# Masked attention of a four-layer network on one core: the order of TensorE's products inside a position, front units cut in two, and a second layer that seeds both pairs

## The chip, the core and the metric

The program runs on one core of a Trainium2 chip. The core has TensorE (PE), which multiplies matrices into PSUM, VectorE (DVE), ScalarE (ACT), GpSimd (POOL), and SyncE (SP), which here only issues DMAs. Each engine works through its own list of instructions in order; semaphores let one wait for another. The metric is the device time of one execution in microseconds (us), lower is better.

## The reference

The network has four layers, each an attention block and a feed-forward block. Batch 8, 512 tokens, width 256, 16 heads of 16. Layers 0, 1 and 3 have a masked cross attention; these three are what the change touches. For each of them:

```
Q = heads(norm(x) @ Wq + bq);  K = heads(ctx @ Wk + bk);  V = heads(ctx @ Wv + bv)
scores = Q @ K^T / sqrt(16)        # layer 1: + adj[query, key]
scores = where(mask == 0, very negative, scores)
x = x + softmax(scores) @ V @ Wo + bo
```

Layers 0 and 1 have a mask for each batch element, layer 3 one mask for all; layer 1 adds a matrix `adj` of floats to the scores.

## The kernel before

`masked_attention` (called three times) keeps x in SBUF and loops over the 8 batch elements ("batches" below; two of them are one turn of a hardware loop, the first and last ones are written out). A batch is cut into NG = 4 groups of GH = 4 heads, and a group into 4 blocks of 128 keys: 16 **steps** s, each with two halves, so 32 **positions** p = 2s + half. Every engine walks the same positions, in `pe_positions`, `dve_positions`, `act_positions`; POOL and SP have a frame for each batch. What stands at a position is fixed by hand.

At each position TensorE does, for two of the four heads:

- two **maxima products** (`p1_ps[0]`, `p1_ps[1]`; L280), 128 queries by 512 keys, seven steps ahead of the rest. VectorE adds the mask and takes the row maximum of each (L452, one instruction and a short read of its accumulator). There are only these two banks: a product may start when the maximum of the product two before it is done (semaphore `maxed`).
- two **score products** (`p2_ps[half]`, L293), 128 keys by 512 queries, with the maximum already subtracted inside the product through three extra rows of `q_stack`. The mask is added in one of three ways. By ACT: it **seeds** the two banks with the mask (`act_seed`, L512) before the product, which adds on top. By PE: two more products with the identity after it (L298), layers 0 and 3. By DVE: it adds the mask while copying to `probs` (L467), layer 1. Then ACT takes the exponential (L535).
- at odd positions the four **value products** of the step before (L308, f32, into `oT_ps`).

Between these stand **front units** in one bank `front_ps`: transposes of the normed x (`xT`), projections `k`, `q`, `v` for a later batch, the output projection `out` of the batch before, and `m`, which turns the maxima of a group (split in three bf16 parts by `dve_split_maxima`) so that they can be put into `q_stack`. The tables `VALUES`, `FRONT`, `TAIL`, `MAXIMA` say at which position; ACT or DVE reads a unit one position later, ahead of its other work there. A batch has 10 units of the five kinds and 4 of `m`.

Which half is seeded by whom, before:

```python
def by_act(s, half):
    return half == 0 or s % 2 == 1
def by_dve(s, half):
    return adj is not None and not by_act(s, half)
def by_pe(s, half):
    return adj is None and not by_act(s, half)
```

So of the 32 position pairs of a batch 24 are seeded by ACT; the eight at half 1 of even steps go by PE (layers 0 and 3) or DVE (layer 1).

The program's own functions follow.

## Time and profile before

| | |
|---|---|
| median of 3 runs | 3940.72 us (3933.82 to 3943.34) |
| the profiled execution's own time | 3939.15 us |
| its span, first to last instruction | 3937.3 us |
| PE busy over the span | 3204.4 us (81%) |
| DVE busy | 2542.3 us (65%) |
| ACT busy | 2278.4 us (58%) |
| POOL busy | 1118.4 us (28%) |
| masked attention of layer 0, 1, 3 | about 60 to 700, 1060 to 1756, 2880 to 3516 us of the span |
| its value products (L308) | 3072, 422.3 us busy |
| its maxima on DVE (L452) | 1536, 1003.9 us busy |

The kernel has stages with different limits, so the shares over the span say little. The change lies in the three stages of masked attention, half of the time. In them the granted clock of TensorE was 0.93 to 0.98 of full speed.

In the rows below, "L280 ... x2" in a timeline is a run of equal instructions merged into one row; the first number is its start in us from the start of the span, the second how long it took. A matmul's duration holds its way through the array, so for the time that it takes from the next one, compare starts. In square brackets stands how long the engine was idle before, and what ended that.

### The profile page before, as it was taken

The page shows a single profiled execution, that of the slowest core. Times are in us where ns is not written, and L with a number is a line of the kernel's source. Part 1 is how long each engine was busy: PE and PEld are TensorE (multiplying, and loading weights), DVE is VectorE, ACT ScalarE, POOL GpSimd, SP SyncE. Part 2 cuts the span into 40 slices and gives each one's busy share as a digit, 9 for nine tenths or more (in the row PEclk, how much of TensorE's full clock was granted, in tenths as well). Part 3 has the DMA queues.
Part 4 walks back from the last instruction along what each step waited for, and adds up shares of the span by engine and source line. Part 5 has one row for each costly group of instructions (what it writes and reads, how often), then busy time and mean ns, then how long its engine had stood idle before and what let it go on. Part 6 is the DMA issues. An engine that isn't in the chain of part 4 may idle for free. (4 is left out here: it accounts for less than half of the span.)

```text
span 3937.3 us, 66613 instructions
## 1 busy us (share of the span) xinstructions
PE 3204.4 (81%) x16721; PEld 1523.3 (39%) x16721; DVE 2542.3 (65%) x7732; ACT 2278.4 (58%) x3034; POOL 1118.4 (28%) x1194
## 2 busy tenths in 40 slices
PE   5888888799578888876997888888379889866897
PEld 2333332344222322224653555555123333225565
DVE  4776776677578788755215777888867777745531
ACT  1887879444177677762114666676538888861111
POOL 3344431000444455401112432331332211101232
PEclk8999999899799999977998999998589999985899
DMA  5322330000343333301007988997031221103242
GB/s 143 82 66 69 84 76 18 22 1 0 100 108 96 89 92 89 84 9 48 0 15 245 305 286 278 312 325 262 24 79 39 49 66 41 34 12 107 69 101 67
DMA packets 212154, 392.83 MB, mean 100 GB/s; under 512 B 24633, under 2 KB 76986, under 8 KB 211658
## 3 DMA queue, kind: packets, MB, share of 16 engines
q1 hardware_dynamic: 168777, 296.38, 27.1%
q10 hardware_dynamic: 36864, 83.90, 5.7%
q0 software_dynamic: 6144, 8.39, 1.3%
q8 instruction: 139, 2.28, 0.2%
q14 instruction: 230, 1.88, 0.2%
HBM read 189.88 MB, written 96.47 MB: 73 GB/s over the span
## 5 line engine op out<-in xcount | busy, mean ns | idle before, releaser
L452 DVE CUSTOM_DVE_ANT_0 A_sums<-A_p_ps,A_bias 128x512 bf16<-128x512 f32 x1536 | 1003.9, 685 | 366.1 <-PE A_p_ps L280 348.8
L535 ACT ACTIVATE A_probs<-A_p_ps 128x1024 f32<-128x1024 f32 x704 | 715.0, 1017 | 191.5 <-PE A_p_ps L293 152.5
L280 PE MATMUL A_p_ps<-A_k_stack,A_q_stack 96*128 96x512 bf16 x1536 | 538.0, 396 | 231.1 <-DVE A_nmax L452 221.9
L512 ACT ACTIVATE A_p_ps<-A_biasT 128x1024 f32<-128x1024 bf16 (+1 forms) x576 | 592.0, 1028 | 73.7 <-ACT A_probs L535 2.9
L293 PE MATMUL A_p_ps<-A_q_stack,A_k_stack 99*128 99x512 bf16 x1536 | 473.6, 391 | 41.2 <-ACT A_p_ps L512 39.2
L308 PE MATMUL A_oT_ps<-A_probs,A_v_aug 128*17 128x512 f32 x3072 | 422.3, 623 | 0.5 <-ACT A_probs L535 0.5
L280 PEld LDWEIGHTS A_p_ps<-A_k_stack,A_q_stack 96*128 96x128 bf16 x1536 | 131.6, 98 | 723.6 <-DVE A_nmax L452 626.0
L1107 DVE CUSTOM_DVE_ANT_0 A_scores<-A_qk_ps,A_rel_in 128x384 f32<-128x384 f32 (+3 forms) x512 | 232.6, 486 | 83.3 <-PE A_qk_ps L991 72.0
L1014 PE MATMUL A_t_ps<-ident,A_scores 128*128 128x128 f32 x1280 | 226.5, 298 | 57.2 <-DVE A_probsT L1097 47.4
L1097 DVE COPY A_probsT<-A_t_ps 128x384 f32<-128x384 f32 (+3 forms) x512 | 229.0, 484 | 54.3 <-PE A_t_ps L1014 45.6
L1162 ACT ACTIVATE A_rel_out<-A_rel_ps 128x1024 f32<-128x1024 f32 (+3 forms) x256 | 180.1, 704 | 141.7 <-PE A_rel_ps L980 132.6
L1169 ACT ACTIVATE A_scores<-A_scores,A_nmax 128x384 f32<-128x384 f32 (+3 forms) x512 | 257.5, 555 | 7.6 <-DVE A_nmax L1107 7.5
L293 PEld LDWEIGHTS A_p_ps<-A_q_stack,A_k_stack 99*128 99x128 bf16 x1536 | 144.3, 99 | 207.2 <-ACT A_p_ps L512 77.2
L1189 POOL TENSOR_SCALAR_AFFINE_SELECT A_rel_in<-A_rel_in 128x256 f32<-128x256 f32 x256 | 102.6, 410 | 386.5 <-DMA A_rel_in<-A_rel_dram 383.8
L1014 PEld LDWEIGHTS A_t_ps<-ident,A_scores 128*128 128x128 f32 x1280 | 151.0, 148 | 133.9 <-DVE A_probsT L1097 56.4
L582 POOL TENSOR_SCALAR A_bias<-A_mask_in 128x512 bf16<-128x512 int32 (+2 forms) x68 | 131.4, 1933 | 217.2 <-DVE A_nmax L452 196.1
L582 POOL TENSOR_SCALAR A_biasT<-A_mask_in 128x512 bf16<-128x512 int32 (+2 forms) x68 | 131.1, 1927 | 205.9 <-DVE A_probs L467 82.5
L1524 PE MATMUL B_cv_ps<-B_hs,B_tap_diag 128*128 128x512 f32 x384 | 179.0, 602 | 2.7 <-DVE B_hs L1626 2.7
L2780 ACT ACTIVATE M_hid<-M_h_ps,M_b 128x512 f32<-128x512 f32 x64 | 44.0, 688 | 189.6 <-PE M_h_ps L2582 189.6
L2099 ACT ACTIVATE U_hid<-U_h_ps,U_hid_bias 128x512 f32<-128x512 f32 x64 | 44.0, 687 | 177.6 <-PE U_h_ps L1937 177.6
L991 PE MATMUL A_qk_ps<-A_k_stack,A_q_stack 96*128 96x384 bf16 (+3 forms) x512 | 126.7, 312 | 13.8 <-DVE A_nmax L1107 12.2
L561 POOL CAST A_parts<-A_qk 128x512 bf16<-128x512 f32 x84 | 51.2, 609 | 297.0 <-ACT A_qk L497 296.6
(345 smaller groups left out, 5407.5 us busy)
## 6 DMA issues: line engine op xcount, KB each, us to landing
A_k_stack<-A_parts SPq DMA_DIRECT2D x192, 256.0 KB, 5.0
A_q_stack<-A_parts SPq DMA_DIRECT2D x192, 256.0 KB, 5.2
A_rel_dram<-A_rel_out ACTq DMA_DIRECT2D x64, 512.0 KB, 5.1
A_rel_in<-A_rel_dram SPq DMA_DIRECT2D x64, 512.0 KB, 5.0
A_rel_dram<-A_rel_out ACTq DMA_DIRECT2D x64, 384.0 KB, 4.1
A_rel_in<-A_rel_dram SPq DMA_DIRECT2D x64, 384.0 KB, 5.2
A_ctxT<-in_ctxT SPq DMA_DIRECT2D x32, 512.0 KB, 6.3
A_mask_in<-in_mask SPq DMA_DIRECT2D x64, 256.0 KB, 4.4
```

The lines of the kernel that those rows point to most:

```text
L280: nc.tensor.matmul(p1_ps[i % 2][:, :], q_stack[0:KS, a_par, j * GH + i, t * P:(t + 1) * P], k_stack[0:KS, a_par, j * GH + i, :], start=Tru ...
L293: last = nc.tensor.matmul(p2_ps[half][:, i % 2, :], k_stack[:, par, j * GH + i, kb * P:(kb + 1) * P], q_stack[:, par, j * GH + i, :], star ...
L308: nc.tensor.matmul(oT_ps[CW * i:CW * i + HD + 1, :], v_aug[:, v_par, kb, j * GH + i, :], probs[:, (s - 1) % 2 * 2 + i // 2, i % 2, :], sta ...
L452: nc.vector.tensor_tensor_reduce(out=sums[:, i % NX, :], in0=p1_ps[i % 2][:, :], in1=bias[:, t, :], scale=-1.0, scalar=3.4028235e38, op0=A ...
L512: nc.scalar.activation(p2_ps[half][:, :, :], turned, ACT.Copy).then_inc(seeded, 1)
L535: nc.scalar.activation(dst, src, ACT.Exp).then_inc(exp_done, 1)
L582: last = nc.gpsimd.tensor_scalar(dst, mask_in[:, k % 2, :], 0.0, NEG, ALU.is_equal, ALU.mult)
L1014: last = nc.tensor.transpose(t_ps[:, i, kb, :], scores[(p - TURN_LAG) % NP][:, i, kb * P:(kb + 1) * P], ident[:, :])
L1097: nc.vector.tensor_copy(probsT[u % NP][:, i, 0:nk, :], t_ps[:, i, 0:nk, :]).then_inc(copied, 1)
L1107: nc.vector.tensor_tensor_reduce(out=scores[p % NP][:, i, 0:n], in0=qk_ps[i][:, 0:n], in1=rel_in[s % NI][:, (2 * half + i) * n:(2 * half + ...
L1162: nc.scalar.activation(rel_out[a % NO][:, 2 * half * n:(2 * half + 2) * n].rearrange("p (i n) -> p i n", i=2), rel_ps[:, :, 0:n], ACT.Copy ...
L1169: nc.scalar.activation(scores[u % NP][:, i, 0:n], scores[u % NP][:, i, 0:n], ACT.Exp, bias=nmax[:, u % NP, i:i + 1], scale=-1.0).then_inc( ...
```

## The change

Four things, all in the masked layers.

1. TensorE's order inside a position. Before: both maxima products, scores, values, front unit. Now: first maxima product, scores, first half of a front unit, an `m` unit if one is due, second maxima product, second half of the front unit, values.
2. A front unit is cut into two pieces of 256 columns (`piece`), and reported as full after the second. `k` and `q` units were products with 512 moving columns and are now twice as many with 256; the others keep their instructions.
3. The tables move: all ten units now stand at even positions (before, `v` 0 and 1 at 1 and 5, `xT` 1 at 15, `q` 0 at 25). `END` goes from 12 to 14 with `out` 1.
4. Layer 1: `by_act` is always true. ACT seeds the eight pairs that DVE used to add the mask to, DVE's addition (L467) and the semaphore `biased` go, and ACT reads scores from PSUM at every position. Layers 0 and 3 keep their eight pairs by PE.

```diff
 def by_act(s, half):
-    return half == 0 or s % 2 == 1
+    return adj is not None or half == 0 or s % 2 == 1
...
-VALUES = [(1, "v", 0), (5, "v", 1)]
-FRONT = [(12, "xT", 0), (15, "xT", 1), (18, "k", 0), (20, "k", 1), (25, "q", 0), (28, "q", 1)]
-TAIL = [(8, "out", 0), (10, "out", 1)]
+VALUES = [(0, "v", 0), (4, "v", 1)]
+FRONT = [(14, "xT", 0), (16, "xT", 1), (20, "k", 0), (22, "k", 1), (24, "q", 0), (28, "q", 1)]
+TAIL = [(8, "out", 0), (12, "out", 1)]
...
 # pe_shared
-for c in range(DC):
-    last = nc.tensor.matmul(front_ps[:, :], wt[:, c, i * P:(i + 1) * P], src[:, c, :],
+cols = slice(piece * D, (piece + 1) * D)
+for c in range(DC):
+    last = nc.tensor.matmul(front_ps[:, cols], wt[:, c, i * P:(i + 1) * P], src[:, c, cols],
                             start=c == 0, stop=c == DC - 1)
...
+if piece == 1:
+    last.then_inc(front_full, 1)
...
 # pe_positions, one position
+if has(b, a):
+    pe_max_unit(pe, b, a, a_par, 2 * half)
+if has(b, s):
+    pe_scores(pe, b, s, half, par)
+for n, kind, i in here:
+    pe_shared(pe, n, kind, i, uses_before(b), b, 0)
+for n, kind, i in shared(plan, p):
+    if kind == "m":
+        pe_maxima(pe, n, i, uses_before(b), b)
+if has(b, a):
+    pe_max_unit(pe, b, a, a_par, 2 * half + 1)
+for n, kind, i in here:
+    pe_shared(pe, n, kind, i, uses_before(b), b, 1)
 if half == 1 and has(b, s - 1):
+    pe_values(pe, b, s, par)
...
 # dve_positions
-if has(b, s) and by_dve(s, half):
-    dve.wait_ge(p2_done, b * HALVES + p + 1).then_inc(apart_dve, 1)
-    nc.vector.tensor_tensor(probs[:, s % 2 * 2 + half, :, :], p2_ps[half][:, :, :], turned, ALU.add).then_inc(biased, 1)
...
 # act_positions: at every position now
+act.wait_ge(p2_done, b * HALVES + p + 1).then_inc(apart_act, 1)
+nc.scalar.activation(probs[:, s % 2 * 2 + half, :, :], p2_ps[half][:, :, :], ACT.Exp).then_inc(exp_done, 1)
```

TensorE in layer 0, batch 0, from position 18 on: `p1_ps` are the maxima banks, `p2_ps` the scores, `oT_ps` the values, `front_ps` the front bank (here a `k` unit and an `m` unit). Before:

```order
L280 MATMUL A0_p1_ps0<-A0_k_stack,A0_q_stack 128x512
L280 MATMUL A0_p1_ps1<-A0_k_stack,A0_q_stack 128x512
L293 MATMUL A0_p2_ps0<-A0_q_stack,A0_k_stack 128x512 x2
L241 MATMUL A0_front_ps<-A0_ctxT,A0_wk 128x512 x2
L280 MATMUL A0_p1_ps0<-A0_k_stack,A0_q_stack 128x512
L280 MATMUL A0_p1_ps1<-A0_k_stack,A0_q_stack 128x512
L293 MATMUL A0_p2_ps1<-A0_q_stack,A0_k_stack 128x512 x2
L308 MATMUL A0_oT_ps<-A0_probs,A0_v_aug 17x512 x4
L252 MATMUL A0_front_ps<-ident_bf,A0_m_parts 12x128 x4
```

After, positions 18, 19 and the start of 20:

```order
L261 MATMUL A0_p1_ps0<-A0_k_stack,A0_q_stack 128x512
L276 MATMUL A0_p2_ps0<-A0_q_stack,A0_k_stack 128x512 x2
L261 MATMUL A0_p1_ps1<-A0_k_stack,A0_q_stack 128x512
L261 MATMUL A0_p1_ps0<-A0_k_stack,A0_q_stack 128x512
L276 MATMUL A0_p2_ps1<-A0_q_stack,A0_k_stack 128x512 x2
L251 MATMUL A0_front_ps<-ident_bf,A0_m_parts 12x128 x4
L261 MATMUL A0_p1_ps1<-A0_k_stack,A0_q_stack 128x512
L292 MATMUL A0_oT_ps<-A0_probs,A0_v_aug 17x512 x4
L261 MATMUL A0_p1_ps0<-A0_k_stack,A0_q_stack 128x512
L276 MATMUL A0_p2_ps0<-A0_q_stack,A0_k_stack 128x512 x2
L230 MATMUL A0_front_ps<-A0_ctxT,A0_wk 128x256 x2
L261 MATMUL A0_p1_ps1<-A0_k_stack,A0_q_stack 128x512
```

The scores moved between the two maxima products, the `m` unit moved from behind the values to ahead of the second maxima product, and the `k` unit went two positions on and is cut: half of it stands ahead of the second product, the other half behind.

ScalarE at the start of layer 1 (`A1_p2_ps0`, `A1_p2_ps1` are the banks of half 0 and 1; L512 seeds, L535 is the exponential). Before:

```order
L535 ACTIVATE A1_probs<-A1_p2_ps0 128x1024
L512 ACTIVATE A1_p2_ps0<-A1_biasT 128x1024
L535 ACTIVATE A1_probs<-A1_probs 128x1024
L512 ACTIVATE A1_p2_ps1<-A1_biasT 128x1024
L535 ACTIVATE A1_probs<-A1_p2_ps0 128x1024
L512 ACTIVATE A1_p2_ps0<-A1_biasT 128x1024
L535 ACTIVATE A1_probs<-A1_p2_ps1 128x1024
```

After (L529 is the exponential):

```order
L529 ACTIVATE A1_probs<-A1_p2_ps0 128x1024
L512 ACTIVATE A1_p2_ps0<-A1_biasT 128x1024
L529 ACTIVATE A1_probs<-A1_p2_ps1 128x1024
L512 ACTIVATE A1_p2_ps1<-A1_biasT 128x1024
L529 ACTIVATE A1_probs<-A1_p2_ps0 128x1024
L512 ACTIVATE A1_p2_ps0<-A1_biasT 128x1024
L529 ACTIVATE A1_probs<-A1_p2_ps1 128x1024
L512 ACTIVATE A1_p2_ps1<-A1_biasT 128x1024
```

Every exponential is now followed by a seed, and none reads `probs` that DVE wrote.

## Rows read from the trace of the kernel before

**Rows 1.** Windows (layers 1, 3): length, busy PE, PEld, DVE, ACT, POOL; clock, DMA

```profile
1060.00:1756.00 696.00, 561.96 (x2557) 184.03 (x2555) 534.21 (x1472) 507.60 (x553) 306.13 (x246) 0.93 0.30 80
2880.00:3516.00 636.00, 553.78 (x2696) 196.81 (x2696) 437.67 (x1378) 505.22 (x554) 133.89 (x136) 0.98 0.19 43
```

**Rows 2.** Timeline of PE in layer 3: a step without a unit, then one

```profile
3205.46 0.61 PE L280 MATMUL A_p_ps<-A_k_stack,A_q_stack 96*128 96x512 bf16 x2
...
3206.80 0.39 PE L280 MATMUL A_p_ps<-A_k_stack,A_q_stack 96*128 96x512 bf16 x1 [0.29 <-DVE A_nmax L452]
3207.41 0.39 PE L280 MATMUL A_p_ps<-A_k_stack,A_q_stack 96*128 96x512 bf16 x1 [0.22 <-DVE A_nmax L452]
3207.64 0.60 PE L293 MATMUL A_p_ps<-A_q_stack,A_k_stack 99*128 99x512 bf16 x2
...
3208.60 1.05 PE L308 MATMUL A_oT_ps<-A_probs,A_v_aug 128*17 128x512 f32 x8
3209.58 1.98 PE L241 MATMUL A_front_ps<-A_xnT,A_wq 128*128 128x512 f32 x4
3211.40 0.60 PE L280 MATMUL A_p_ps<-A_k_stack,A_q_stack 96*128 96x512 bf16 x2
```

**Rows 3.** Timeline in layer 3: from a maxima product to its maximum and back

```profile
3187.45 0.60 PE L280 MATMUL A_p_ps<-A_k_stack,A_q_stack 96*128 96x512 bf16 x2
...
3188.02 0.69 DVE L452 CUSTOM_DVE_ANT_0 A_sums<-A_p_ps,A_bias 128x512 bf16<-128x512 f32 x1 [1.30 <-PE A_p_ps L280]
...
3188.78 0.39 PE L280 MATMUL A_p_ps<-A_k_stack,A_q_stack 96*128 96x512 bf16 x1 [0.30 <-DVE A_nmax L452]
```

**Rows 4.** Timeline of ACT in layer 3: seed, exponential, seed

```profile
3189.82 1.03 ACT L512 ACTIVATE A_p_ps<-A_biasT 128x1024 f32<-128x1024 bf16 x1
3190.79 1.02 ACT L535 ACTIVATE A_probs<-A_p_ps 128x1024 f32<-128x1024 f32 x1
3191.93 1.03 ACT L512 ACTIVATE A_p_ps<-A_biasT 128x1024 f32<-128x1024 bf16 x1
```

**Rows 5.** Timeline of ACT: the `oT_ps` copy, a batch apart (layers 3, 1)

```profile
3175.73 0.58 ACT L524 ACTIVATE A_oT_sb<-A_oT_ps 128x512 f32<-128x512 f32 x1
...
3252.20 0.58 ACT L524 ACTIVATE A_oT_sb<-A_oT_ps 128x512 f32<-128x512 f32 x1
...
1378.11 0.58 ACT L524 ACTIVATE A_oT_sb<-A_oT_ps 128x512 f32<-128x512 f32 x1
...
1461.77 0.58 ACT L524 ACTIVATE A_oT_sb<-A_oT_ps 128x512 f32<-128x512 f32 x1
...
1543.65 0.58 ACT L524 ACTIVATE A_oT_sb<-A_oT_ps 128x512 f32<-128x512 f32 x1
```

**Rows 6.** The same copy, one group apart, in layer 3's last batch

```profile
3421.68 0.58 ACT L524 ACTIVATE A_oT_sb<-A_oT_ps 128x512 f32<-128x512 f32 x1
...
3437.75 0.58 ACT L524 ACTIVATE A_oT_sb<-A_oT_ps 128x512 f32<-128x512 f32 x1
```

**Rows 7.** Timeline of DVE in layer 3: second maximum of a position, split's end

```profile
3192.85 0.68 DVE L452 CUSTOM_DVE_ANT_0 A_sums<-A_p_ps,A_bias 128x512 bf16<-128x512 f32 x1
...
3193.67 0.19 DVE L406 TENSOR_TENSOR A_m_parts<-A_m_rest,A_m_parts 128x16 bf16<-128x16 f32 x1
```

**Rows 8.** Timeline of PE, layer 3: a whole `v` unit

```profile
3228.48 2.00 PE L247 MATMUL A_front_ps<-A_wv,A_ctxT 128*128 128x256 f32 x8
```

**Rows 9.** Groups by line, layer 3: the weight loads of the `v` units

```profile
L247 PEld LDWEIGHTS A_front_ps<-A_wv,A_ctxT 128*128 128x128 f32 x112 | 20.8, 195 | 13.7 <-issue 11.3
```

**Rows 10.** Waits of ACT in layer 1, longest first: us in total, times, longest

```profile
ACT A_probs L535 <- DVE A_probs L467: 84.4, 59, 4.0
```

**Rows 11.** Waits of PE: in us, times, longest; layer 1, then layer 3

```profile
PE A_p_ps L280 <- DVE A_nmax L452: 94.5, 198, 2.3
PE A_p_ps L293 <- ACT A_p_ps L512: 23.7, 40, 2.4
...
PE A_p_ps L280 <- DVE A_nmax L452: 64.2, 197, 1.0
```

More of the change, by code:

```diff
@@ L173, in masked_attention @@
         START = 7
-        END = 12
+        END = 14
         def plan_of(b):
@@ new lines, in pe_max_unit, with pe_scores @@
+        def pe_max_unit(pe, b, a, a_par, i):
+            unit = (b * STEPS + a) * GH + i
+            _, _, j, t = ahead(a - LEAD)
+            if later(unit - 1):
+                pe.wait_ge(maxed, unit - 1)
+            nc.tensor.matmul(p1_ps[i % 2][:, :], q_stack[0:KS, a_par, j * GH + i, t * P:(t + 1) * P],
+                             k_stack[0:KS, a_par, j * GH + i, :], start=True, stop=True).then_inc(p1_done, 1)
+        def pe_scores(pe, b, s, half, par):
+            j, kb = s // TPB, s % TPB
+            pair = (2 * half, 2 * half + 1)
+            if half == 0 and kb == 0:
+                pe.wait_ge(m_placed[j % 2], (b * (NG // 2) + j // 2 + 1) * GH * 16)
+            if every_mask and s < TPB and not by_act(s, half):
+                pe.wait_ge(bias_ready, b * MK + TPB + kb + 1)
+            if by_act(s, half):
+                pe.wait_ge(seeded, seeds(b, s, half))
+            elif later(b * STEPS + s):
+                pe.wait_ge(exp_done, b * HALVES + 2 * s + half - 1)
+            for i in pair:
+                last = nc.tensor.matmul(p2_ps[half][:, i % 2, :], k_stack[:, par, j * GH + i, kb * P:(kb + 1) * P],
+                                        q_stack[:, par, j * GH + i, :], start=not by_act(s, half), stop=by_act(s, half),
+                                        skip_group_check=by_act(s, half))
+            if not by_act(s, half):
+                for i in pair:
+                    last = nc.tensor.matmul(p2_ps[half][:, i % 2, :], ident_bf[:, :], biasT[:, kb, :],
+                                            start=False, stop=True)
+            last.then_inc(p2_done, 1)
@@ new lines, in pe_values @@
+        def pe_values(pe, b, s, par):
+            j, kb = (s - 1) % STEPS // TPB, (s - 1) % TPB
+            v_par = par if s else 1 - par
+            pe.wait_ge(exp_done, b * HALVES + 2 * s)
+            if kb == 0 and later(b * NG + (s - 1) // TPB):
+                pe.wait_ge(oT_read, b * NG + (s - 1) // TPB)
+            for i in range(GH):
+                nc.tensor.matmul(oT_ps[CW * i:CW * i + HD + 1, :], v_aug[:, v_par, kb, j * GH + i, :],
+                                 probs[:, (s - 1) % 2 * 2 + i // 2, i % 2, :],
+                                 start=kb == 0, stop=kb == TPB - 1).then_inc(pv_done, 1)
@@ L311, in pe_positions @@
-                for n, kind, i in shared(plan, p):
-                    pe_shared(pe, n, kind, i, uses_before(b), b, par)
+                a_par = (par + over) % 2
+                if has(b, a) and half == 0 and a % STEPS == 0:
+                    for stack in stack_ready:
+                        pe.wait_ge(stack, (b + over + 1) * SLOTS * 16)
+                here = [(n, kind, i) for n, kind, i in shared(plan, p) if kind != "m"]
+                if has(b, a):
+                    pe_max_unit(pe, b, a, a_par, 2 * half)
```

112 lines of the change are left out of this document (25 added, 87 removed).

## The prediction

> **What bounds the kernel now.** I read first the windows of the masked layers, since the shares over the whole span mix stages: in layer 3 PE is busy 553.8 of 636 us and ACT 505.2, in layer 1 PE 562.0, DVE 534.2 and ACT 507.6 of 696 [rows 1]. No engine is full, so the limit is a mix of PE's work and of waits between engines. The waits of PE name the partner: 64.2 us in layer 3 and 94.5 in layer 1 for a maximum on DVE, against 23.7 for a seed of ACT in layer 1 [rows 11].
>
> The timeline of a step without a front unit shows the mechanism [rows 2]. From 3205.46, where its even position starts, to 3209.58, where its values have been issued, it takes 4.12 us. PE's own issue in it is less. A product of 512 columns takes 0.23 from start to start (3207.41 to 3207.64); two scores and two mask products take 0.96 (to 3208.60), the values 0.98 (to 3209.58). Four maxima products, two more scores, 0.96 and 0.98 are 3.27 us at 0.22 each. The other 0.85 are waits: a maxima product may start only when DVE is done with the product two before. That round trip is read from three rows: the product is issued at 3187.45, its maximum starts on DVE at 3188.02 (0.57), and 0.76 later, at 3188.78, PE issues into the freed bank [rows 3]. So a bank turns in 1.33 us, and DVE's pitch is 0.67 to 0.69 for one maximum. A bare even position (two maxima, two scores) is only 0.88 long. The first maxima product of the odd position waits 0.45 for the 1.33; the second stands right behind it and waits again until the next maximum is done, 0.69 later: 0.45 more, less rounding. By this count a bare step is 4.10 us, where the trace has 4.12. A front unit at the even position, 1.82 long (3209.58 to 3211.40 for one at an odd position [rows 2]), covers this wait; one at an odd position doesn't.
>
> A whole batch takes 76.47 us in layer 3 (3175.73 to 3252.20), in layer 1 83.66 and 81.88, mean 82.8 [rows 5].
>
> **The change, layers 0 and 3.** (a) With the new order the second maxima product comes 0.66 behind the first, at the pace of DVE, and finds its bank free. The first one of the odd position still waits 0.45. A bare step falls by 0.4.
>
> (b) By the tables, the steps with no unit of 1.8 us at their even position are ten now (0 to 3, 7, 8, 11, 12, 13, 15): 10 x 0.85 = 8.5 us of waits. After, they are 1, 3, 5, 9, 13, 15 at 0.45, and 7 and 8, where a short `xT` unit brings the even position to about 1.3, at nothing: 2.7. That removes 5.8 us from a batch.
>
> (c) Given back: the `m` unit now stands ahead of a maxima product instead of behind the values. It needs the end of the split. From the start of the second maximum to that end is 3193.67 + 0.19 - 3192.85 = 1.01 [rows 7]; that maximum starts 1.36 after the even position's start, so the unit may start at 2.43. PE is there at 1.33 + 0.22 + 0.5 = 2.05. A wait of 0.4, four times: 1.6. Before, the values (0.98) stood there and hid it; queued behind it now are the second maxima product, which DVE waits for, and the values.
>
> (d) ACT becomes late where PE no longer is. Seed to exponential is 0.97, exponential to the next seed 1.14 [rows 4]. A step with two seeds is 2 x 2.11 = 4.2 and a copy of some 0.5 (the 0.58 of [rows 5], less overlap). Step 8 is shorter than that on PE (about 3.75), steps 10 and 14 about equal: 1.0 together.
>
> (e) The cuts. PE goes from bf16 to f32 and back twice as often; about 0.08 is what 0.96 has over four products of 0.22, where PE changes to f32 [rows 2]. Ten more changes at half of that: 0.5.
>
> (f) `k` and `q` units have twice the weight loads. I cost them at nothing: a `v` unit, eight products of 256 columns, takes 2.00 [rows 8], a `q` unit, four of 512, takes 1.98 [rows 2]; the cover is the product in flight. Without cover it would be one load of 0.195 [rows 9] for each.
>
> The Trainium skill ("TensorE: Matmul & The Clock Gate", section "The mechanism" of Part 3) says that a weight load overlaps products in flight only if it goes to another group of rows. Here all loads of a unit use all 128 rows; by that rule the `v` unit's eight loads would add 1.6 us to its products, and the trace doesn't show them.
>
> Sum for a batch: -5.8 + 1.6 + 1.0 + 0.5 = -2.7; the waits behind DVE's other work (norm, heads, splits) I take as unchanged. Six batches of each of the two layers have front units: 12 x 2.7 = 32 us. The last two batches have fewer. A group there takes 16.07 [rows 6], where ACT's own work is six seeds with their exponentials at 2.11, two single exponentials of about 1.0 and two copies at 0.5: 15.7. That leaves 0.4 to gain in a group, 16 x 0.4 = 6 us. Together 38.
>
> **Layer 1.** DVE loses 64 additions, for which ACT waited 84.4 us [rows 10]; ACT gains 64 seeds of 0.97 to 1.14. ACT then has 32 x 2.11 = 67.5 in a batch and 14 copies at 0.5: 74.5, more than PE (no mask products: eight times 0.43 less than in layer 3). It is the bound. Where single steps on PE are still longer (an even step with unit, 4.7 against 4.2) and round DVE's heavy stretch (norm, two heads, `out` at positions 6 to 9) I add 4: 78.5, against 82.8 now. 6 x 4.3 = 26 us; in the last two batches, already short, nothing. The bounds are 0 and 82.8 - 74.5 = 8.3 for a batch.
>
> **Total:** 38 + 26 = 64 us less than the profiled execution's 3939.15 is 3875; the median of the runs lies 1.6 above it, so I say 3877.
>
> **Rivals.**
> *Everything removed stays removed* (chance 0.16). If splits are ready and ACT smooths its load over neighbouring steps, (c) to (e) vanish: 5.8 x 12 + 6 = 76, and layer 1 at 76.5 gives 38. That is 114 us: 3827. For it: steps with much ACT work stand beside ones with little. Against: each score product needs its own seed, so ACT can be late by one position at most.
> *Given back in full* (0.08). DVE's heavy stretch had a unit at position 10 behind it, which gave DVE 1.8 us to catch up; now positions 9 to 11 are bare. If that and the split cost 2.5 more for a batch in all three layers, about 45 are lost: 3922 or more, down to no difference.
> *The weight loads are not hidden* (0.04). 28 units of `k` and `q` in the loops of each layer, four more loads each: 84 x 4 x 0.195 = 66 us. Then 3943: no gain. Against it speaks (f). By the rule of the Trainium skill named in (f) it is this case that would come.
> *Slower: the second maxima product queues behind the scores* (0.08). A score product that waits for its seed now holds up half of DVE's supply; before, both maxima products were ahead of it. PE waited for seeds only 40 times, 23.7 us, in layer 1 [rows 11], but with ACT as the bound there it would wait at nearly all positions, and PE gets to the scores 0.22 earlier than before. A maximum that is late by w makes the next position late by up to w. Over 768 positions it costs 768 w; at w = 0.08 us the gain is gone, at 0.12 it gives 3877 + 92 = 3969. Against: from the end of a seed to the moment when ACT wants that score lie an exponential and a seed, 2.1 us, and PE needs about 0.7 for the scores.
>
> **How the numbers follow.** The forecast, 3850 to 3910, has 0.64. The range reaches from the first rival (3827, and a little of it is left out below) into the second: 3828 to 3926. Above lie the last two and part of the second, together about 0.16. A change within 0.3% (12 us) can hardly be told from none here. Faster: 0.64 + 0.16 + a third of the second, 0.83. Same: the rest of the second and the third, 0.09. Slower: 0.08.
>
> **What would show it.** Right: PE's waits for a maximum fall by more than half in all three layers, and a bare step shows one such wait, not two; the batch in layer 3 is at 73.8; `k` and `q` units cut in two are 0.9 + 0.9 long; in layer 1 ACT is the busiest, with the batch at 78.5 and no exponential waiting for DVE. Wrong: PE's waits move to the seeds (scores) and to the split (`m` unit) with sizes above 0.4; DVE is idle as long as before; weight loads show between the halves; the stretch round positions 6 to 11 grows by more than what the bare steps give.

## The result, and the profile after

| | before | after |
|---|---|---|
| median of the runs on one chip | 3938.4 us (3933.82 to 3943.34) | 3868.81 us (3864.12 to 3871.64) |
| ratio, 95% interval | | 0.9822 [0.9805, 0.9839] |
| span of the profiled execution | 3937.3 us | 3862.4 us |
| PE, DVE, ACT busy | 3204.4, 2542.3, 2278.4 us | 3166.3, 2497.0, 2330.4 us |

The change makes the kernel 70 us faster (1.8%); 64 was predicted. Medians and ratios here and below are those of executions in the faster of the chip's two states; one execution of the kernel before, at 4764.6 us, was in the slower one. The windows of layers 1 and 3, with the columns of [rows 1]:

```profile
1021.00:1695.00 674.00, 552.30 (x2672) 211.00 (x2672) 470.31 (x1413) 566.71 (x617) 310.66 (x248) 0.93 0.31 84
2820.00:3442.00 622.00, 550.47 (x2808) 218.37 (x2808) 453.67 (x1378) 501.70 (x554) 131.38 (x135) 0.97 0.19 44
```

Both stages are shorter. In layer 1 ACT is now the busiest (566.7 of 674), as forecast; DVE lost 64 us there. In layer 3 PE and ACT are as busy as before. DVE is busy for 16 us more (437.7 to 453.7): 11 of them are at the maxima (335.0 to 346.0), which take as long each (686 and 687 ns, about 351 us for all 512) but whose records overlap less now that they no longer follow each other directly, and the rest are other instructions of DVE that lasted longer.

To split the 75 us of the span by stage I take ScalarE's copies of `oT_ps`, 32 in each masked layer, one for each group. Here are the first and the last of layer 1 and of layer 3 after the change:

```profile
1077.61 0.58 ACT L524 ACTIVATE A_oT_sb<-A_oT_ps 128x512 f32<-128x512 f32 x1
1694.20 0.60 ACT L524 ACTIVATE A_oT_sb<-A_oT_ps 128x512 f32<-128x512 f32 x1 [1.25 <-PE A_oT_ps L292]
2879.16 0.58 ACT L524 ACTIVATE A_oT_sb<-A_oT_ps 128x512 f32<-128x512 f32 x1
3441.32 0.60 ACT L524 ACTIVATE A_oT_sb<-A_oT_ps 128x512 f32<-128x512 f32 x1 [1.25 <-PE A_oT_ps L292]
```

From the first to the last copy layer 1 takes 616.6 us and layer 3 562.2. The same marks in both traces give:

| from mark to mark | before | after | difference |
|---|---|---|---|
| start of the span to layer 0's first | 114.4 | 105.5 | -8.9 |
| layer 0, first to last | 585.8 | 557.2 | -28.6 |
| on to layer 1's first | 417.2 | 414.9 | -2.3 |
| layer 1 | 638.3 | 616.6 | -21.7 |
| on to layer 2's first | 395.2 | 393.0 | -2.2 |
| layer 2 (not changed) | 611.4 | 617.3 | +5.9 |
| on to layer 3's first | 181.7 | 174.7 | -7.0 |
| layer 3 | 571.2 | 562.2 | -9.0 |
| on to the end | 422.1 | 421.1 | -1.0 |

A stage moves by 3 to 7 us between kernels that have the same code in it: layer 2 lay between 611.1 and 618.3 in all traces of this study, and among six kernels with the same code in layers 0 and 3, layer 0 lay between 555.8 and 558.7 and layer 3 between 555.4 and 559.6. Differences of that size are not read as effects. Below, a kernel's "length of layer 0, 1, 3" is this first-to-last length in its profiled execution.

Every fourth copy begins another batch. The mean of the first six batches, and the length of the last two together, in us:

| | layer 0 | layer 1 | layer 3 |
|---|---|---|---|
| a batch, mean of six, before | 79.4 | 85.9 | 76.8 |
| after | 74.6 | 82.3 | 75.3 |
| the last two together, before | 109.5 | 123.1 | 110.6 |
| after | 109.5 | 123.0 | 110.6 |

All that the masked layers gained lies in the first six batches.

PE's waits in layer 1 after the change (us in total, times, longest), against [rows 11]:

```profile
PE A_p_ps L261 <- DVE A_nmax L460: 41.1, 79, 2.1
PE A_p_ps L276 <- ACT A_p_ps L512: 33.0, 43, 1.5
PE A_front_ps L251 <- DVE A_m_parts L414: 27.8, 20, 2.7
PE A_front_ps L230 <- ACT A_m_row L490: 9.1, 7, 2.1
```

And in layer 3:

```profile
PE A_p_ps L261 <- DVE A_nmax L460: 35.4, 77, 1.5
PE A_p_ps L276 <- ACT A_p_ps L512: 10.3, 16, 1.5
PE A_front_ps L251 <- DVE A_m_parts L414: 9.9, 23, 1.1
...
PE A_front_ps L230 <- ACT A_m_row L490: 5.2, 6, 0.9
```

The waits for a maximum fell by 57% in layer 1 (94.5 to 41.1) and by 45% in layer 3 (64.2 to 35.4), in number from 198 and 197 to 79 and 77. A part came back: as waits of the `m` unit for the split, in layer 1 for seeds, and as waits of a front unit that stands directly behind an `m` unit until ACT has read the bank (between the first and the last copy of layer 3, all kinds of units together, 7.4 us against 0.4 before). The timeline of a step without a unit in layer 3 after the change, with the start of the next one:

```profile
3151.86 0.39 PE L261 MATMUL A_p_ps<-A_k_stack,A_q_stack 96*128 96x512 bf16 x1
3152.08 0.60 PE L276 MATMUL A_p_ps<-A_q_stack,A_k_stack 99*128 99x512 bf16 x2
3152.52 0.38 PE L261 MATMUL A_p_ps<-A_k_stack,A_q_stack 96*128 96x512 bf16 x1
3153.19 0.39 PE L261 MATMUL A_p_ps<-A_k_stack,A_q_stack 96*128 96x512 bf16 x1 [0.29 <-DVE A_nmax L460]
...
3153.85 0.38 PE L261 MATMUL A_p_ps<-A_k_stack,A_q_stack 96*128 96x512 bf16 x1
3154.16 1.05 PE L292 MATMUL A_oT_ps<-A_probs,A_v_aug 128*17 128x512 f32 x8
3155.56 0.39 PE L261 MATMUL A_p_ps<-A_k_stack,A_q_stack 96*128 96x512 bf16 x1 [0.35 <-DVE A_nmax L460]
```

Inside the step there is one wait, at the first maxima product of the odd position, where [rows 2] had two. The second product of each position starts without one. (This step has no mask products, the one of [rows 2] has them.)

### The profile page after: what moved, and what is told of

It reads as the page before. It is cut to its first block and busy times, and to the rows that moved or that the text cites. A ratio compares the mean times of both kernels' runs of the same rounds, so it can differ in the third digit from the quotient of the medians.

```text
span 3862.4 us, 67385 instructions
## 1 busy us (share of the span) xinstructions
PE 3166.3 (82%) x17105; PEld 1598.6 (41%) x17105; DVE 2497.0 (65%) x7668; ACT 2330.4 (60%) x3098; POOL 1118.6 (29%) x1194
## 5 line engine op out<-in xcount | busy, mean ns | idle before, releaser
L460 DVE CUSTOM_DVE_ANT_0 A_sums<-A_p_ps,A_bias 128x512 bf16<-128x512 f32 x1536 | 1036.0, 687 | 443.7 <-PE A_p_ps L261 405.2
L529 ACT ACTIVATE A_probs<-A_p_ps 128x1024 f32<-128x1024 f32 x768 | 777.7, 1015 | 175.5 <-PE A_p_ps L281 76.7
L512 ACT ACTIVATE A_p_ps<-A_biasT 128x1024 f32<-128x1024 bf16 (+1 forms) x640 | 657.6, 1028 | 77.9 <-ACT A_probs L529 3.7
L261 PE MATMUL A_p_ps<-A_k_stack,A_q_stack 96*128 96x512 bf16 x1536 | 603.4, 395 | 119.9 <-DVE A_nmax L460 112.0
L261 PEld LDWEIGHTS A_p_ps<-A_k_stack,A_q_stack 96*128 96x128 bf16 x1536 | 149.4, 97 | 646.0 <-DVE A_nmax L460 562.3
L1100 DVE CUSTOM_DVE_ANT_0 A_scores<-A_qk_ps,A_rel_in 128x384 f32<-128x384 f32 (+3 forms) x512 | 232.4, 486 | 88.2 <-PE A_qk_ps L984 82.8
```

The costliest lines, as they stand in the source:

```text
L261: nc.tensor.matmul(p1_ps[i % 2][:, :], q_stack[0:KS, a_par, j * GH + i, t * P:(t + 1) * P], k_stack[0:KS, a_par, j * GH + i, :], start=Tru ...
L460: nc.vector.tensor_tensor_reduce(out=sums[:, i % NX, :], in0=p1_ps[i % 2][:, :], in1=bias[:, t, :], scale=-1.0, scalar=3.4028235e38, op0=A ...
L512: nc.scalar.activation(p2_ps[half][:, :, :], turned, ACT.Copy).then_inc(seeded, 1)
L529: nc.scalar.activation(probs[:, s % 2 * 2 + half, :, :], p2_ps[half][:, :, :], ACT.Exp).then_inc(exp_done, 1)
L1100: nc.vector.tensor_tensor_reduce(out=scores[p % NP][:, i, 0:n], in0=qk_ps[i][:, 0:n], in1=rel_in[s % NI][:, (2 * half + i) * n:(2 * half + ...
```

## The experiments

All were run in five rounds, in turn with the kernel before: the first four of the list below the change beside a median of before of 3936.5 us, the next four beside 3939.7, the last four beside 3940.3 (the change itself beside 3938.4). Medians, ratios to before with their 95% intervals, and the lengths of the three layers:

| kernel | median us | ratio | layer 0 | layer 1 | layer 3 |
|---|---|---|---|---|---|
| before | 3938.4 | | 585.8 | 638.3 | 571.2 |
| the change | 3868.8 | 0.9822 [0.9805, 0.9839] | 557.2 | 616.6 | 562.2 |
| seed_only | 3917.6 | 0.9949 [0.9932, 0.9967] | 584.8 | 618.0 | 574.2 |
| dve_adds | 3970.6 | 1.0085 [1.0065, 1.0105] | 563.3 | 704.2 | 565.8 |
| old_order | 3871.0 | 0.9836 [0.9811, 0.9860] | 562.4 | 613.1 | 563.4 |
| old_tables | 3881.4 | 0.9856 [0.9833, 0.9878] | 566.1 | 605.8 | 573.4 |
| m_last | 3855.1 | 0.9792 [0.9764, 0.9819] | 556.6 | 613.5 | 559.6 |
| uncut | 3864.8 | 0.9806 [0.9781, 0.9831] | 556.2 | 617.5 | 558.9 |
| cut_c | 3865.5 | 0.9816 [0.9791, 0.9841] | 560.6 | 619.3 | 562.8 |
| m_last_l1old | 3839.3 | 0.9746 [0.9719, 0.9772] | 556.0 | 592.5 | 555.5 |
| nan_late_l1old | 3836.3 | 0.9748 [0.9727, 0.9769] | 558.7 | 591.9 | 555.5 |
| q_late | 3847.5 | 0.9766 [0.9746, 0.9787] | 556.5 | 609.8 | 555.4 |
| v_late | 3845.0 | 0.9760 [0.9739, 0.9781] | 556.5 | 600.0 | 555.5 |
| nan_late | 3855.1 | 0.9788 [0.9767, 0.9809] | 555.8 | 611.1 | 555.4 |

Across these groups I compare ratios, and medians only within one.

### The seeding alone, and all but the seeding

`seed_only` is the kernel before with one line of the change (and without POOL's wait for `biased`, which nothing raises any more):

```diff
-return half == 0 or s % 2 == 1
+return adj is not None or half == 0 or s % 2 == 1
```

> The kernel before with nothing but layer 1's seeding changed. Theory A: about 26 us faster than the kernel before, about 3912, all in layer 1, where ACT becomes the busiest engine. Rival: with the old order, ACT as the bound and PE waiting for maxima add up, and nothing is gained (3935 to 3942).

`dve_adds` is the changed kernel with that line as it was (and DVE's addition, its semaphore and POOL's wait for it back):

```diff
-return adj is not None or half == 0 or s % 2 == 1
+return half == 0 or s % 2 == 1
```

> The changed kernel with layer 1's eight pairs of a batch added by VectorE again (L467 back, ACT seeds 24). Theory A: layer 1 gives back the 26 us that the prediction gave it, about 3895; layers 0 and 3 don't move. Rival: layer 1's gain is the order's, and the 64 seeds on ACT cost as much as the 64 additions on VectorE did: within 5 us of the changed kernel, or faster.

Alone, the seeding shortens layer 1 by 20 us (638.3 to 618.0). But with the new order and without the seeding, layer 1 takes 704.2, which is 88 longer than after the change and 66 longer than before, and the kernel is slower than before. Its waits in layer 1:

```profile
ACT A_probs L553 <- DVE A_probs L485: 148.7, 59, 5.9
PE A_p_ps L271 <- DVE A_nmax L470: 75.4, 66, 5.5
PE A_p_ps L286 <- ACT A_p_ps L530: 64.3, 63, 2.8
```

ACT waits 148.7 us for DVE's additions, against 84.4 before [rows 10]. DVE makes the addition behind the second maximum of the position, and TensorE now issues that product behind the scores; when a score product waits for its seed, the second maximum, the addition, the exponential and the next seed all come later, one after the other. PE's waits for seeds are 64.3 us, against 23.7 before [rows 11]. (The longest single wait, 5.9 us, is no example of it: 3.0 of it are idle time of DVE ahead of the addition for which the trace shows no reason.) This fits the chain that I had as the slower rival, and with the seeding layer 1 doesn't show it: two parts of the change that looked separate are not. That it is the new order that does this, and not the new places, is argued from the lists; no run has DVE's additions with only one of the two.

### The order and the tables, one without the other

`old_order` is the changed kernel with both maxima products first and the pieces of a unit back to back behind the values, with the `m` unit after them:

```diff
 if has(b, a):
     pe_max_unit(pe, b, a, a_par, 2 * half)
+    pe_max_unit(pe, b, a, a_par, 2 * half + 1)
 if has(b, s):
     pe_scores(pe, b, s, half, par)
-for n, kind, i in here:
-    pe_shared(pe, n, kind, i, uses_before(b), b, 0)
...
-if has(b, a):
-    pe_max_unit(pe, b, a, a_par, 2 * half + 1)
-for n, kind, i in here:
-    pe_shared(pe, n, kind, i, uses_before(b), b, 1)
 if half == 1 and has(b, s - 1):
     pe_values(pe, b, s, par)
+for n, kind, i in here:
+    for piece in range(2):
+        pe_shared(pe, n, kind, i, uses_before(b), b, piece)
...
```

> The changed kernel with TensorE's old order inside a position: both maxima products, scores, values, the two halves of the front unit back to back, the m unit. Tables and seeding stay new. Theory A (the change pays by sparing waits for a maximum on VectorE): each bare step has its second wait of about 0.4 us again, eight of them in a batch, and the m unit's wait of about 0.4 (four in a batch) goes; about 25 us slower than the changed kernel, near 3894, with PE's waits for a maximum back above 50 us in each layer. Theory B (the new places of the units do nearly all of it): at most 5 us slower. Theory C (seeding in layer 1 does nearly all): layers 0 and 3 as in the changed kernel.

`old_tables` is the changed kernel with the places of before:

```diff
-VALUES = [(0, "v", 0), (4, "v", 1)]
-FRONT = [(14, "xT", 0), (16, "xT", 1), (20, "k", 0), (22, "k", 1), (24, "q", 0), (28, "q", 1)]
-TAIL = [(8, "out", 0), (12, "out", 1)]
-END = 14
+VALUES = [(1, "v", 0), (5, "v", 1)]
+FRONT = [(12, "xT", 0), (15, "xT", 1), (18, "k", 0), (20, "k", 1), (25, "q", 0), (28, "q", 1)]
+TAIL = [(8, "out", 0), (10, "out", 1)]
+END = 12
```

> The changed kernel with the old places of the front units (and END 12). Order, cuts and seeding stay new. Theory A: steps whose even position is bare are ten again, at 0.45 us each instead of six at 0.45 and two at nothing: 1.8 us for a batch, 18 batches, some 25 to 30 us slower than the changed kernel, about 3896. Theory B (places do nearly all): 40 us or more slower in layers 0 and 3 together. Rival: order alone does it, at most 5 us slower.

From `seed_only` (0.9949) the order alone (with the cuts and the `m` unit's move) leads to 0.9856, the tables alone to 0.9836, both to 0.9822: 37, 45 and 50 us of some 3940. So the two are largely substitutes; the 5 us between 45 and 50 are within the intervals. Of the theories for `old_order`, A (25 us slower) fell and B's number came (at most 5 slower, 5.5 by the ratios), but not as B reads it, since the places aren't needed for most of the gain: the order alone gives 37. `old_tables` is 13 us slower by the ratios, half of its theory A.

Each of the two puts PE's other work into the gap that DVE needs between maxima, and a gap can be filled once. PE's waits for a maximum between the first and the last copy of layer 3 show this: 54.1 us in `seed_only`, 30.4 with the order alone, 40.3 with the tables alone, 27.0 with both. But in layer 3 the order alone brings only 1 us of time (574.2 to 573.4), the tables 11 (to 563.4), although the order takes away more of these waits. `old_tables` has others in their place, in layer 3:

```profile
PE A_p_ps L261 <- DVE A_nmax L460: 30.4, 88, 1.0
...
PE A_front_ps L251 <- ACT A_qk L497: 9.3, 6, 1.6
PE A_front_ps L251 <- DVE A_m_parts L414: 8.3, 14, 1.3
PE A_front_ps L251 <- DVE x_sb L394: 5.1, 7, 1.1
```

The `m` unit (L251) comes earlier in the new order, while the old places put `out` 1 and `k` 0 directly ahead of it: it waits 14.4 us for their bank to be read and 8.3 for the split, 22.7 of the 23.7 us that the maxima gave. So in layer 3 the order's small gain may be a matter of the bank and not of the gap; the old places with the `m` unit behind the values were run in layer 1 only (`m_last_l1old`). In layer 0 the order brings 19, the tables 22, both 28. In layer 1 the old places are better by 11 us than the new ones (605.8 against 616.6): there this part of the change seems to cost time, and the runs below make it clearer.

### The two halves of a unit

`uncut` issues the whole front unit behind the second maxima product:

```diff
-for n, kind, i in here:
-    pe_shared(pe, n, kind, i, uses_before(b), b, 0)
...
 for n, kind, i in here:
-    pe_shared(pe, n, kind, i, uses_before(b), b, 1)
+    for piece in range(2):
+        pe_shared(pe, n, kind, i, uses_before(b), b, piece)
```

> The changed kernel with the whole front unit in one place, behind the second maxima product and ahead of the values (the products of k and q units still 256 wide). My theory, that what the order brings comes from the scores between two maxima products and not from the cut: within 8 us of the changed kernel (3861 to 3877). Rival: the half unit ahead of the second maxima product is what gives DVE its evenly spaced products; then PE's waits for a maximum grow at each of the 10 units of a batch by up to 0.4 us, 3 layers x 7 batches x 10 x 0.4 = 84 at most, and some 3890 to 3950 comes out.

`cut_c` cuts `k` and `q` by the contraction instead of by columns, so that each half needs two weight loads, not four:

```diff
-for c in range(DC):
-    last = nc.tensor.matmul(front_ps[:, cols], wt[:, c, i * P:(i + 1) * P], src[:, c, cols],
+for c in (piece,):
+    last = nc.tensor.matmul(front_ps[:, :], wt[:, c, i * P:(i + 1) * P], src[:, c, :],
```

> The changed kernel with k and q units cut by the contraction instead of by columns: each half is two products of 512 columns for one of the two blocks of weights, so the unit loads weights as often as before the change (half as often as in the changed kernel). My theory, step f: the extra weight loads lie hidden under the product in flight, so the time is that of the changed kernel within 5 us and a unit takes 1.7 to 1.8 us of PE's issue either way. Rival, the loads are not hidden: 84 units x 4 loads x 0.195 us = 66 us faster, about 3803.

Both intervals hold the changed kernel's 0.9822, and no layer is more than 3.4 us away from its. Cutting the units brought nothing that can be measured, and the doubled weight loads cost nothing. A `k` unit after the change, with the second maxima product between its halves (layer 3):

```profile
3133.09 1.03 PE L230 MATMUL A_front_ps<-A_ctxT,A_wk 128*128 128x256 f32 x4
3133.95 0.38 PE L261 MATMUL A_p_ps<-A_k_stack,A_q_stack 96*128 96x512 bf16 x1
3134.17 1.03 PE L230 MATMUL A_front_ps<-A_ctxT,A_wk 128*128 128x256 f32 x4
3135.03 0.38 PE L261 MATMUL A_p_ps<-A_k_stack,A_q_stack 96*128 96x512 bf16 x1
```

The same unit in `cut_c`, with products of 512 columns:

```profile
3133.72 1.02 PE L230 MATMUL A_front_ps<-A_ctxT,A_wk 128*128 128x512 f32 x2
3134.58 0.38 PE L261 MATMUL A_p_ps<-A_k_stack,A_q_stack 96*128 96x512 bf16 x1
3134.80 1.02 PE L230 MATMUL A_front_ps<-A_ctxT,A_wk 128*128 128x512 f32 x2
3135.66 0.38 PE L261 MATMUL A_p_ps<-A_k_stack,A_q_stack 96*128 96x512 bf16 x1
```

0.86 from start to start for a half in either, with four loads or with two.

### The `m` unit behind the values again

`m_last`:

```diff
-for n, kind, i in shared(plan, p):
-    if kind == "m":
-        pe_maxima(pe, n, i, uses_before(b), b)
...
 if half == 1 and has(b, s - 1):
     pe_values(pe, b, s, par)
+for n, kind, i in shared(plan, p):
+    if kind == "m":
+        pe_maxima(pe, n, i, uses_before(b), b)
```

> The changed kernel with one thing moved: the m unit stands behind the values again, as before the change, and no longer ahead of the second maxima product. My theory (step c of the prediction, mis-sized for layer 1): PE's 49 us of waits for the split's end (11, 28 and 10 in layers 0, 1, 3) go nearly all, and the rest of the path gets some of it: layers 0 and 3 are 5 to 10 us shorter each, layer 1 about 15, and the total is 3840 to 3850. Rival: the time that PE waits there is time in which DVE catches up, so PE's waits for a maximum grow by as much as those for the split fall, and the total stays at 3869 within 5.

12 us faster than the change by the ratios (0.9792 against 0.9822; the intervals overlap; the five later kernels built on it agree on layers 0 and 3: 555.8 to 558.7, 555.4 to 555.5). PE's waits in layer 1:

```profile
PE A_p_ps L261 <- DVE A_nmax L460: 46.0, 77, 2.1
...
PE A_front_ps L230 <- ACT A_m_row L490: 10.3, 8, 2.1
PE A_front_ps L235 <- ACT A_m_row L490: 6.7, 5, 2.0
PE A_front_ps L242 <- ACT A_m_row L490: 5.0, 4, 2.0
PE A_front_ps L251 <- DVE A_m_parts L414: 0.6, 1, 0.6
```

Those for the split are gone, as the theory had it (25.1 us in the same window after the change, 0.6 here). Nearly all of them came back: 14 us at the maxima products (31.6 to 46.0) and 8 at front units that now find the bank not yet read (13.7 to 22.0). In layer 1 the rival was nearer: the layer is 3 us shorter, not 15, which is within what a stage moves by itself. Layer 3 gains 3 to 7 us, layer 0 at most 1.4 where 5 to 10 were expected; in total the 12 us lie between theory and rival.

### Where layer 1 loses by the new places

`m_last_l1old` has the old places in layer 1 alone:

```diff
 TAIL = [(8, "out", 0), (12, "out", 1)]
+if adj is not None:
+    VALUES = [(1, "v", 0), (5, "v", 1)]
+    FRONT = [(12, "xT", 0), (15, "xT", 1), (18, "k", 0), (20, "k", 1), (25, "q", 0), (28, "q", 1)]
+    TAIL = [(8, "out", 0), (10, "out", 1)]
...
-END = 14
+END = 14 if adj is None else 12
```

> The kernel with the m unit behind the values, and in layer 1 alone the old places of the front units (END 12 there too). In the run with the old places in all three layers, layer 1 was 11 us shorter than in the changed kernel and layer 3 was 11 us longer. If that holds and adds to the move of the m unit, layer 1 is 8 to 12 us shorter than in the run with the m unit moved alone, and the rest is the same. Rival: the 11 us were the split's lateness, which the moved m unit already takes away; then layer 1 is within 3 us of that run.

Layer 1 is 21 us shorter (613.5 to 592.5), twice what I expected, and a batch takes 78.5 in the mean of six, what I had predicted for the change. The first suspect was a row of DVE in `m_last`, one of the three small instructions on rows without any key:

```profile
1194.17 1.24 DVE L420 TENSOR_SCALAR A_nan_rows<-A_nmax 128x4 f32<-128x4 f32 x1
```

POOL at that moment:

```profile
1194.12 1.27 POOL L578 TENSOR_TENSOR A_biasT<-A_biasT,A_adj_in 128x512 f32<-128x512 f32 x1
```

Four elements in a row take 1.24 us, and they end with POOL's addition (1195.41 and 1195.39). In `m_last_l1old` the mean of the seven is 0.32. Three runs test whether that is the 21 us. `q_late` moves one unit in layer 1, so that it stands between the two; `v_late` moves the two `v` units; `nan_late` moves nothing but the three DVE instructions, to position 28, where POOL is idle.

In this order:

```diff
+if adj is not None:
+    FRONT[4] = (25, "q", 0)
```

```diff
+if adj is not None:
+    VALUES = [(1, "v", 0), (5, "v", 1)]
```

```diff
-if i == pair[0] and adj is not None and split % NG == 0:
-    dve_all_masked(dve, b + split // NG, (par + split // NG) % 2)
+first = group_split(b, p - 2) if p >= 2 else None
+if first is not None and adj is not None and first % NG == 0:
+    dve_all_masked(dve, b + first // NG, (par + first // NG) % 2)
```

> The kernel with the m unit behind the values, and in layer 1 alone the unit q 0 at position 25 instead of 24. Where the 21 us of layer 1 went that the old places gave (613.5 to 592.5): my theory is a collision of VectorE with POOL. POOL's addition of adj to a mask block is released by the scores of position 25 and lasts 1.27 us; three small VectorE instructions on the maxima (all-masked rows) come at position 26. With q 0 at 24 nothing lies between the two and the first of them lasts 1.2 us, with q 0 at 25 it lasts 0.32, since the unit's 1.9 us stand between. By this theory the one number brings that instruction down to 0.2 to 0.4 us and layer 1 by 1 to 2 us in each of 6 batches, 6 to 12 of the 21 us. Rival: the gain comes from the k or v units' places; then layer 1 stays at 613 within 3.

> The kernel with the m unit behind the values, and in layer 1 alone the v units at positions 1 and 5 instead of 0 and 4. Theory: by the collision this changes nothing at position 26, so layer 1 keeps most of the 21 us (above 604). Rival: with no mask products on PE in layer 1, ACT is the bound there, and a unit at an odd position fills the wait before a maxima product; then each v unit gives about 1 us, 12 us in the layer, and layer 1 is at 602 or below.

> The kernel with the m unit behind the values, and nothing moved on TensorE or ScalarE: only VectorE's three small instructions on all-masked rows (layer 1 alone has them) come two positions later, at 28, where POOL is idle. Theory, the collision with POOL's addition: each of them lasts 0.17 to 0.2 us there instead of 1.24, 0.17 and 0.41; the maximum queued behind them comes 1.5 us earlier in each of 7 batches, and layer 1 is 6 to 12 us shorter than 613.5. Rival, the lateness of that maximum is made up elsewhere or the length is of the instruction itself: durations fall or not, but layer 1 stays within 3 us.

`nan_late_l1old` is the last of these edits on top of `m_last_l1old`.

> The same three instructions two positions later, on top of the old places of the front units in layer 1. There they already last 0.17 to 0.32 us, so by the theory of the collision nothing is left to gain: layer 1 at 592.5 within 3 us and the total at 3839 within 6. Rival, that their place in VectorE's list costs by itself whatever they last: layer 1 falls by another 3 us or more here as well.

The instruction's duration follows the collision as expected: least, median and longest of seven in ns, in `m_last`

```profile
L420 DVE TENSOR_SCALAR A_nan_rows<-A_nmax x7: 1078/1233/1252, 1113.1 to 1599.6; 128x4 f32<-128x4 f32 x7
```

and in `nan_late`

```profile
L420 DVE TENSOR_SCALAR A_nan_rows<-A_nmax x7: 164/166/166, 1121.1 to 1602.6; 128x4 f32<-128x4 f32 x7
```

But layer 1 falls by 2.4 us, not by 6 to 12, and `nan_late_l1old` changes nothing. My theory of the cost fell: the collision is there, and the path hardly feels it. `q_late` gives 3.7, with that instruction at 0.51 in the mean and not at 0.2 to 0.4; both falls are within what a stage moves by itself. `v_late` gives 13.5 of the 21 us and leaves that instruction at 1.24: the rival's number came (600.0, at 602 or below). Its reason, a filled wait ahead of a maxima product, doesn't show: PE's waits for a maximum in layer 1 are 46.0 us in `m_last` and 48.7 in `v_late`. What changed is the bank. In `m_last` the `v` unit at position 4 stands directly behind the `m` unit of position 3 in the one front bank. PE:

```profile
1218.09 0.39 PE L251 MATMUL A_front_ps<-ident_bf,A_m_parts 128*12 128x128 bf16 x4
...
1220.62 1.13 PE L235 MATMUL A_front_ps<-A_wv,A_ctxT 128*128 128x256 f32 x4 [1.08 <-ACT A_m_row L490]
1221.58 0.38 PE L261 MATMUL A_p_ps<-A_k_stack,A_q_stack 96*128 96x512 bf16 x1
```

DVE's next maximum:

```profile
1222.15 0.69 DVE L460 CUSTOM_DVE_ANT_0 A_sums<-A_p_ps,A_bias 128x512 bf16<-128x512 f32 x1 [2.16 <-PE A_p_ps L261]
```

The `v` unit waits 1.08 for ACT to read the `m` unit; ACT, the bound of this layer, comes to it late, behind a seed. In the new order half of the unit stands ahead of the second maxima product, so DVE is idle for 2.16. At position 5 both maxima products of position 4 and the first of position 5 go ahead of it. PE's waits for the bank before `v` units are 6.7 us in `m_last` and none in `v_late`, and ACT's waits for scores fall from 23.8 to 13.3. That is one place of the two; why `v` 0 at position 1 is better than at 0, and how the rest of the 21 us divides, no run tells.

## Why the prediction was right, point by point

**The total** was 64; the medians say 70. Within the marks, layers 0 and 3 together gave 37.6 against 38, layer 1 21.7 against 26. The agreement in layers 0 and 3 is partly luck: 28.6 and 9.0, where I had 19 each. The mechanism held in kind: the waits for a maximum fell, ACT became the bound of layer 1, and the terms (c) and (d) were given back where I had them. The sizes of single terms didn't hold, one term was missing (see (b)), and the range was wide enough for their sum. Of the signs that I had named, "fall by more than half in all three layers" came for the time in layer 1 only (45% in layer 3, 46% in layer 0: 63.2 to 34.1); the sign for being wrong, "DVE is idle as long as before", did not come (198 to 168 us in the windows of layer 3).

**(a) The bare step** shows one wait, not two, as said. The row gives it as 0.29, but it counts from the modelled end of the product before; counted as in the prediction, from start to start less 0.22, it is 3153.19 - 3152.52 - 0.22 = 0.45, what I had. There is another before the next even position, 0.35 in the row, where I had none: DVE was then at its addition of heads (L361), which took 1.20 us in this place.

**(b) The tables.** Starts of every fourth position's first maxima product, median of six batches in layer 3, give this; units in brackets:

| positions | 0-3 | 4-7 | 8-11 | 12-15 | 16-19 | 20-23 | 24-27 | 28-31 | sum |
|---|---|---|---|---|---|---|---|---|---|
| before | 10.58 (v) | 10.04 (v) | 10.65 (out, out) | 8.30 (xT, xT) | 9.16 (k) | 8.85 (k) | 9.91 (q) | 8.97 (q) | 76.5 |
| after | 9.14 (v) | 8.79 (v) | 10.64 (out) | 8.50 (out, xT) | 8.01 (xT) | 10.89 (k, k) | 9.88 (q) | 8.71 (q) | 74.6 |

The batch falls by 1.9 by these medians, by 1.5 in the mean of the six, where I had 2.7; it is at 74.6 (75.3), not at 73.8. The step that failed is the sentence that the waits behind DVE's other work stay unchanged. Positions 8 to 11 hold one unit less (1.7 us of PE) and last as long as before. PE after the change, positions 10 and 11 and the start of 12 (4.70 us):

```profile
2951.49 0.39 PE L261 MATMUL A_p_ps<-A_k_stack,A_q_stack 96*128 96x512 bf16 x1
...
2953.55 0.39 PE L261 MATMUL A_p_ps<-A_k_stack,A_q_stack 96*128 96x512 bf16 x1 [1.02 <-DVE A_nmax L460]
...
2954.56 0.39 PE L251 MATMUL A_front_ps<-ident_bf,A_m_parts 128*12 128x128 bf16 x4 [0.19 <-DVE A_m_parts L414]
...
2956.19 0.39 PE L261 MATMUL A_p_ps<-A_k_stack,A_q_stack 96*128 96x512 bf16 x1
```

Before, the same stretch with an `out` unit in it took 4.75, free of a wait at position 11; the last row is the start of position 12:

```profile
3019.12 0.61 PE L280 MATMUL A_p_ps<-A_k_stack,A_q_stack 96*128 96x512 bf16 x2
...
3020.00 1.89 PE L261 MATMUL A_front_ps<-A_wo,A_heads_outT 128*128 128x256 f32 x8
3021.72 0.60 PE L280 MATMUL A_p_ps<-A_k_stack,A_q_stack 96*128 96x512 bf16 x2
...
3023.87 0.78 PE L280 MATMUL A_p_ps<-A_k_stack,A_q_stack 96*128 96x512 bf16 x2
```

That is the mechanism of the second rival (DVE's heavy stretch needs a unit behind it) at 1.7 us for a batch instead of 2.5. In the other positions the waits fell by 76.5 - 10.65 + 1.7 - (74.6 - 10.64) = 3.6, net of (c) to (e). A term that the sum didn't have at all is the front bank: units directly behind an `m` unit wait for ACT to read it, 7.4 us in layer 3 against 0.4, 1.0 for a batch.

**(c)** The `m` unit waits 23 times for the split, 9.9 us in layer 3: 1.4 for a batch, 1.6 predicted. In layer 1 it is 27.8 us, over twice as much. Every fourth group's split there has the three instructions on rows without any key in it, the first of which takes 1.24 beside POOL's addition; the seven waits behind these splits are 1.3 to 2.6 long and 15.5 us together. `m_last` shows that less than a third of such waits is on the path: some 43 us of them between the first and last copies of the three layers went (9.6, 25.1 and 8.5), and the layers are 6 us shorter, 10 with layer 3 as in the later kernels; the ratios say 12.

**(d), (e)** PE's waits for seeds grew from 7.5 to 10.3 us in layer 3, 0.4 for a batch; 1.0 was too much. The changes of type have no price that shows.

**(f)** held: 66 us for the loads are excluded by `cut_c`, which has half of them and the same time. The sentence of the Trainium skill ("TensorE: Matmul & The Clock Gate", section "The mechanism" of Part 3) that a load overlaps products in flight only when its row group differs doesn't describe this trace, where all loads of a unit use 128 rows. The same section also lets a load into the background weight buffer go ahead of products in flight, which would fit; no run here shows the buffer itself, and I had left it out of the prediction.

**Layer 0** gained 19 us more than layer 3, and I had them equal. Before, its positions 0 to 3 took 12.14, in layer 3 10.58; after, 9.64 and 9.14. A part is a collision that the marks of layer 3 have less of: the last instruction of the split, 16 elements in a row, lasts as long as POOL's addition beside it. DVE in the trace of before, layer 0:

```profile
172.18 2.28 DVE L406 TENSOR_TENSOR A_m_parts<-A_m_rest,A_m_parts 128x16 bf16<-128x16 f32 x1
```

POOL at that moment:

```profile
172.07 2.35 POOL L552 TENSOR_TENSOR x_sb<-x_sb,A_bo_bc 128x1024 f32 x1
```

PE's `m` unit then waited for it:

```profile
174.52 0.39 PE L252 MATMUL A_front_ps<-ident_bf,A_m_parts 128*12 128x128 bf16 x4 [1.10 <-DVE A_m_parts L406]
```

The mean of that instruction between the marks was 0.539 us before in layer 0 and 0.341 in layer 3, and is 0.187 in both after: the positions moved it away from POOL. Its 30 rows between the marks are 16.2 us in layer 0 and 10.2 in layer 3, so their own length accounts for at most 6 of the 19. No experiment put it back, so what of the 19 it is stays open, and the rest has no cause shown; `nan_late` warns that such a row may cost far less than it shows.

**Layer 1.** ACT became the bound, and no exponential waits for DVE, as said. The batch was to be 78.5; the mean of six is 82.3. That the gain (21.7 against 26) is still near the forecast is luck: the two batches of [rows 5] that gave me 82.8 for before were among the shorter ones, and the mean of six was 85.9. So the forecast missed the batch after by 3.8 and the batch before by 3.1, the same way. What was missing in 78.5 the later kernels show: 81.2 with the `m` unit behind the values (`m_last`), 79.2 with the `v` units moved as well (`v_late`), 78.5 with all old places (`m_last_l1old`).

**The last two batches** of layers 0 and 3 were 6 us of the sum. They gave 0.1 together (in the table of batches above, 109.5 and 110.6 before and after): the 0.4 left over ACT's own work in a group wasn't there to gain.

**The openings** had no term. Each masked layer begins with a stretch ahead of its first copy; the three gave 8.9, 2.3 and 7.0. They aren't steady: six kernels with the same layer 0 had their first copy between 105.5 and 110.6, so 4 to 9 us of the first is the change. The one ahead of layer 3 lay between 173.2 and 180.6 in the twelve kernels with the new order or the new places, and at 181.7 and 182.0 without. What in it does that wasn't looked into. Without the openings the 75 us of the span would have been 57, 7 below the forecast.

**The slower rival** (0.08) was wrong for the change. `dve_adds` comes out slower, as it had it, with the waits of its chain, and there they cost more than all gains.

## What to carry to other kernels

Don't add up two edits that fill the same gap of a partner engine: try each alone, since here the order brought 37 us, the places 45, and both 50. When a unit is moved away from a stretch in which the partner is behind, its time isn't gained there, it turns into a wait; look at what lies beside the partner's longest work first. A unit that needs a shared bank should not stand directly behind one that the bound engine still has to read, and least of all ahead of the product that feeds a third engine: moving two such units by one position gave 13.5 us here. When a forecast rests on one period of a loop, read all its periods first; here two of six batches gave a base that was 3 us short.
